# Node products in three fp32r passes, value copies on ScalarE, row sums on GpSimd, in a graph network kernel

## The reference, cut to what matters

```python
xn = layernorm(x)                                   # x: 12500 nodes x 256
h_src, h_dst = xn @ W_src, xn @ W_dst               # 4 heads of 64
a_src = sum_c(h_src * att_src); a_dst = sum_c(h_dst * att_dst)
e = leaky_relu(a_src[src] + a_dst[dst])             # 200000 edges, sorted by dst
alpha = segment_softmax(e, dst)
gat = prelu(layernorm(segment_sum(alpha * h_src[src], dst) + bias))
q, k, v = xn @ Wq, xn @ Wk, xn @ Wv                 # 8 heads of 32
Q, K = elu(q) + 1, elu(k) + 1
KV, Ks = sum_nodes(K^T v), sum_nodes(K)             # linear attention
mix = xn + mlp_and_norms((Q @ KV) / (Q . Ks), xn)
x = x + gat + mix
y = layernorm(x)
w = softmax(mean(y) @ Wr + br)                      # 8 experts
x = x + sum_e w[e] * ffn_e(y)                       # three 256x256 layers each
```

## Time and profile before

| | us |
|---|---|
| median of three runs | 4765.23 |
| lowest, highest run | 4764.68, 4774.9 |
| the profiled execution, its own time | 4775.0 |
| its span, first to last instruction | 4773.2 |
| TensorE busy | 4267.7 (89%) |
| VectorE busy | 3908.7 (82%) |
| ScalarE busy | 2264.6 (47%) |
| GpSimd busy | 1813.6 (38%) |
| mean granted TensorE clock | 0.944 of full speed |

### The profile page before, as it was taken

The page is one execution under the profiler, slowest core; times in us unless marked ns, Lnnn a source line. Parts: engine busy times, 40 slices in busy tenths (PEclk is TensorE's granted clock), DMA queues, the critical chain, the costliest instruction groups (busy, mean ns, idle before and its releaser), DMA issues. The chain is left out here.

```text
span 4773.2 us, 85825 instructions
## 1 busy us (share of the span) xinstructions
PE 4267.7 (89%) x22703; PEld 3319.2 (70%) x22704; DVE 3908.7 (82%) x10182; ACT 2264.6 (47%) x4194; POOL 1813.6 (38%) x1677
## 2 busy tenths in 40 slices
PE   8994888888888888888888885999999999999999
PEld 5663566666666656666666553788888888888888
DVE  7765888888888899888988986877778778778776
ACT  3331343343333343333333432666666666666666
POOL 0007777777777677776776750000000000000000
PEclk9996999998999899999998987999999999999999
DMA  5444766766666667666766663100000000000000
GB/s 189 152 135 138 202 194 202 210 197 190 198 209 199 191 195 216 200 197 187 217 204 191 195 184 110 38 28 15 28 28 14 28 22 21 28 15 28 28 15 19
DMA packets 440121, 603.08 MB, mean 126 GB/s; under 512 B 41544, under 2 KB 366672, under 8 KB 439888
## 3 DMA queue, kind: packets, MB, share of 16 engines
q1 hardware_dynamic: 360016, 378.46, 25.0%
q0 software_dynamic: 79872, 221.62, 17.3%
HBM read 312.66 MB, written 287.25 MB: 126 GB/s over the span
## 5 line engine op out<-in xcount | busy, mean ns | idle before, releaser
L817 POOL DMA_INDIRECT acc<-h_tab,strips x1664 | 1810.6, 1088 | 1028.5 <-issue 830.3
L1316 PE MATMUL ps<-acc 128*128 128x260 f32 x3328 | 991.9, 427 | 48.3 <-DVE acc L936 29.1
L951 DVE SCALAR_TENSOR_TENSOR acc<-acc,strips,ps 128x260 f32<-128x260 f32 x1664 | 796.5, 479 | 231.2 <-PE ps L1316 144.0
L1316 PEld LDWEIGHTS ps<-acc 128*128 128x128 f32 x3328 | 634.5, 208 | 195.5 <-issue 102.2
L936 DVE TENSOR_TENSOR acc<-acc 128x512 f32<-128x512 f32 x832 | 564.3, 683 | 0.0
L1818 ACT ACTIVATE exp<-ps,bn 128x512 f32<-128x512 f32 (+1 forms) x400 | 310.2, 776 | 510.9 <-PE ps L1885 507.3
L1135 ACT ACTIVATE strips<-ps 128x512 bf16<-128x512 bf16 x416 | 247.5, 595 | 428.7 <-PE ps L1292 424.7
L1883 PE MATMUL ps<-w_hi,b_hi 128*128 128x256 f32 x1568 | 444.9, 284 | 1.2 <-DVE exp L1722 1.2
L1885 PE MATMUL ps<-w_hi,b_lo 128*128 128x256 f32 x1568 | 443.6, 283 | 0.0
L1884 PE MATMUL ps<-w_lo,b_hi 128*128 128x256 f32 x1568 | 443.6, 283 | 0.0
L1730 DVE TENSOR_TENSOR a_lo<-exp,a_hi 128x512 fp32r<-128x512 f32 (+1 forms) x400 | 262.0, 680 | 183.4 <-ACT a_hi L1820 169.8
(11 more groups left out here) (256 smaller groups left out, 8116.7 us busy)
## 6 DMA issues: line engine op xcount, KB each, us to landing
side_tab<-acc SPq DMA_DIRECT2D x416, 520.0 KB
acc<-h_tab,strips POOLq DMA_INDIRECT x1664
strips<-xnt_tab SPq DMA_DIRECT2D x50, 512.0 KB
h_tab<-acc SPq DMA_DIRECT2D x25, 520.0 KB, 6.6
exp<-side_tab SPq DMA_DIRECT2D x100, 130.0 KB, 2.3
acc<-in_x SPq DMA_DIRECT2D x25, 512.0 KB, 5.3
base_tab<-acc SPq DMA_DIRECT2D x25, 512.0 KB, 3.2
xnt_tab<-acc SPq DMA_DIRECT2D x25, 512.0 KB, 6.0
```

The source lines that it names most:

```text
L817: pool.indirect_dma_start(G[s][:, b * GU + u], None, h_tab, bass.IndirectOffsetOnAxis(REC[s][:, b * GU + u, 0:1], 0)).then_inc(g_in[s], 16)
L951: nc.vector.scalar_tensor_tensor(A[:, (b % 2) * GU + u], A[:, (k - 1) % (2 * GU) if k else 2 * GU], smt[s][:, k:k + 1], ps[u][:, 0:MW], AL ...
L1316: nc.tensor.matmul(ps[u][:, 0:MW], S32[b % 2][:, u], G[s][:, b * GU + u], start=True, stop=True).then_inc(g_mm.sem, 1)
```

## The change

1. `products` multiplies high and low parts: xh·wh + xh·wl + xl·wh, each fp32r, so six products of each width instead of two per tile. ScalarE writes the high part of the transposed chunk right after the full one (which is still stored for the edge stage); VectorE writes the low part (`turned_low`), and the products wait for it. The weights are split once at the start: two copies on ScalarE, two subtractions on VectorE.
2. The copy of v into `VX` moves from VectorE to ScalarE, between relu k and h.
3. The addition for `XB` moves from VectorE to GpSimd, one per chunk as before. SyncE's base store waits for it, and so does the scaling two chunks on.
4. Order: the halves are transposed after tiles 0 and 1 instead of 1 and 2. The comparisons go from tile 0 to tile 3 and their counts into the following chunk. A segment is closed one chunk later, and the last segment and the joining come after tile 1 of the last chunk.
5. Memory: `acc` becomes a smaller area for weights (`keep`), one for the first stage and, in its place afterwards, one for the edge stage.

The diff, cut to its core:

```diff
             def scale(c):
                 s = c % 2
                 x_tr.wait(dve, c - 2)
+                x_base.wait(dve, c - 2)
...
                 ins.then_inc(x_norm.sem, 1)
-                x_norm.wait(dve, c)
-                used(dve, st_x[s], 16, c // 2)
-                nc.vector.tensor_tensor(XB[s], X[s], XN[s], ALU.add).then_inc(x_base.sem, 1)
+
+            def turned_low(c, k):
+
+                xt_ev.wait(dve, c, k + 1)
+                hk_mm.wait(dve, c - 2)
+                nc.vector.tensor_tensor(XTL[c % 2][:, k], XT[c % 2][:, k], XTH[c % 2][:, k].bitcast(f32),
+                                        ALU.subtract).then_inc(xt_lo.sem, 1)
...
+            for i, part in enumerate((slice(C_K, C_END), slice(C_H, C_K))):
+                dve.wait_ge(wch_set, i + 1)
+                nc.vector.tensor_tensor(WCL[:, :, part], wcat[:, :, part], WCH[:, :, part].bitcast(f32), ALU.subtract
+                                        ).then_inc(wcl_set, 1)
+            for k in range(KD):
+                turned_low(0, k)
             statistics(1)
             root(1)
             scale(1)
...
                     kv_mm.wait(dve, c - 1, t + 1)
                     k_act.wait(dve, c, t + 1)
-                    nc.vector.tensor_copy(VX[:, t, :, 0:P],
-                                          ps[4 + t % 2][:, D:2 * D].rearrange("p (g c) -> p g c", g=KD)
-                                          ).then_inc(v_ev.sem, 1)
                     nc.vector.scalar_tensor_tensor(KK[:, t], KE[:, t], 1.0, KR[:, t], ALU.min,
                                                    ALU.add).then_inc(k_dve.sem, 1)
-                    if t == 0:
+                    if t == 0 and c + 2 < NCH:
+                        statistics(c + 2)
+                    if t == 1 and c + 2 < NCH:
+                        root(c + 2)
+                    if t in (1, 2) and c + 1 < NCH:
+                        turned_low(c + 1, t - 1)
+                    if t == 2 and c + 2 < NCH:
+                        scale(c + 2)
+                    if c and c % SEG_TURNS == 0 and t == (1 if c == nseg * SEG_TURNS else CH - 1):
+                        segment(c // SEG_TURNS - 1)
+                        if c == nseg * SEG_TURNS:
+                            steps_joined()
+                    if t == CH - 1:
                         for k in compared(c):
                             compare(c // SEG_TURNS, k)
-                        if c + 2 < NCH:
-                            statistics(c + 2)
-                    if t == 1 and c + 2 < NCH:
-                        root(c + 2)
-                    if t == 2 and c + 2 < NCH:
-                        scale(c + 2)
-                    if t == CH - 1:
-                        if c % SEG_TURNS == SEG_TURNS - 1 and c < nseg * SEG_TURNS:
-                            segment(c // SEG_TURNS)
-                        if c == nseg * SEG_TURNS - 1:
-                            steps_joined()
...
                 hk_mm.wait(act, c - 2)
+                xt_lo.wait(act, c - 2)
                 x_tr.wait(act, c, k + 1)
-                nc.scalar.activation(XT[c % 2][:, k], ps[k][:, :], ACT.Copy).then_inc(xt_ev.sem, 1)
+                nc.scalar.activation(XT[c % 2][:, k], ps[k][:, :], ACT.Copy)
+                nc.scalar.activation(XTH[c % 2][:, k], ps[k][:, :], ACT.Copy).then_inc(xt_ev.sem, 1)
...
+            act.wait_ge(w_in, 16 * (KD + 4))
+            for i, part in enumerate((slice(C_K, C_END), slice(C_H, C_K))):
+                if i:
+                    act.wait_ge(fold_set, 4 * KD)
+                nc.scalar.activation(WCH[:, :, part], wcat[:, :, part], ACT.Copy).then_inc(wch_set, 1)
+                if i == 0:
+                    for k in range(KD):
+                        turned(0, k)
...
                     nc.scalar.activation(KR[:, t], ps[4 + t % 2][:, 0:D], ACT.Relu).then_inc(k_act.sem, 1)
+                    kv_mm.wait(act, c - 1, t + 1)
+                    nc.scalar.activation(VX[:, t, :, 0:P], ps[4 + t % 2][:, D:2 * D].rearrange("p (g c) -> p g c", g=KD),
+                                         ACT.Copy).then_inc(v_ev.sem, 1)
...
-                    if t in (1, 2) and c + 1 < NCH:
-                        turned(c + 1, t - 1)
+                    if t in (0, 1) and c + 1 < NCH:
+                        turned(c + 1, t)
...
             def products(c, t):

                 pc, pt = (c, t - 2) if t >= 2 else (c - 1, t + 2)
-                xt_ev.wait(pe, c)
+                xt_lo.wait(pe, c)
...
                 for lo, hi, bank in ((C_H, C_K, 2), (C_K, C_END, 4)):
+                    o = ps[bank + t % 2][:, 0:hi - lo]
                     for k in range(KD):
-                        ins = nc.tensor.matmul(ps[bank + t % 2][:, 0:hi - lo], XT[c % 2][:, k, t * P:(t + 1) * P],
-                                               wcat[:, k, lo:hi], start=k == 0, stop=k == KD - 1)
+                        xh, xl = (x[c % 2][:, k, t * P:(t + 1) * P] for x in (XTH, XTL))
+                        wh, wl = WCH[:, k, lo:hi], WCL[:, k, lo:hi]
+                        nc.tensor.matmul(o, xh, wh, start=k == 0, stop=False)
+                        nc.tensor.matmul(o, xh, wl, start=False, stop=False)
+                        ins = nc.tensor.matmul(o, xl, wh, start=False, stop=k == KD - 1)
...
-            pe.wait_ge(w_in, 16 * (KD + 4))
-            pe.wait_ge(fold_sum, 2 * KD)
+            pe.wait_ge(wcl_set, 2)
...
-                    if t in (1, 2) and c + 1 < NCH:
-                        turned(c + 1, t - 1)
-                    if t == 2:
+                    if t in (0, 1) and c + 1 < NCH:
+                        turned(c + 1, t)
+                    if c and t == (0 if c == nseg * SEG_TURNS else 2):
                         if record_turn(c) is not None:
                             rec_ev.wait(pe, record_turn(c))
-                        for k in compared(c):
-                            counts(c // SEG_TURNS, k)
+                        for k in compared(c - 1):
+                            counts((c - 1) // SEG_TURNS, k)
...
+                for c in range(NCH):
+                    s = c % 2
+                    x_norm.wait(pool, c)
+                    pass_on(pool, "pool")
+                    used(pool, st_x[s], 16, c // 2)
+                    nc.gpsimd.tensor_tensor(XB[s], X[s], XN[s], ALU.add).then_inc(x_base.sem, 1)
```

More of the change, by code:

```diff
@@ L138, in build, with rounded @@
         early = ExitStack()
-        acc_t = early.enter_context(nc.sbuf_tensor("acc", [P, 25000], f32))
-        strip_t = early.enter_context(nc.sbuf_tensor("strips", [P, 12288], f32))
+        keep_t = early.enter_context(nc.sbuf_tensor("keep", [P, 4360], f32))
+        strip_t = early.enter_context(nc.sbuf_tensor("strips", [P, 8192], f32))
         work_t = early.enter_context(nc.sbuf_tensor("work", [P, 12088], f32))
+        first = ExitStack()
+        proj_t = first.enter_context(nc.sbuf_tensor("proj", [P, 16840], f32))
+        def rounded(name, n):
+            return first.enter_context(nc.sbuf_tensor(name, [P, KD * n], f32r))[:, :].rearrange("p (k n) -> p k n", k=KD)
+        XTH, XTL = [[rounded(f"xt_{v}{s}", CT) for s in range(2)] for v in ("hi", "lo")]
+        WCH, WCL = rounded("wc_hi", C_END), rounded("wc_lo", C_END)
         ps = [es.enter_context(nc.psum_tensor(f"ps{i}", [P, 512], f32)) for i in range(8)]
@@ L165, in build @@
         RSQ = 12
-        r1 = Region(acc_t)
+        r1 = Region(keep_t)
         kvx = r1.take(KD, P + HH)
@@ L173, in build @@
         w2 = r1.take(2 * KD, D)
-        r2_from = r1.at
+        r1 = Region(proj_t)
         wcat = r1.take(KD, C_END)
         wdst = r1.take(KD, D)
-        fold = r1.take(2, KD, D)
         X = [r1.take(CH, D) for _ in range(2)]
@@ L183, in build @@
         KE = r1.take(CH, D)
+        fold = KE.rearrange("p (s k) d -> p s k d", k=KD)
         KR = r1.take(CH, D)
@@ L205, in build @@
         kv_all, kv_cp, ad_set = sem("kv_all"), sem("kv_cp"), sem("ad_set")
+        wch_set, wcl_set, xt_lo = sem("wch_set"), sem("wcl_set"), stage("xt_lo", 2)
         x_v = a["x"].rearrange("(c t p) d -> c p t d", t=CH, p=P)
@@ L248, in compared @@
             return range(KC * j // SEG_TURNS, KC * (j + 1) // SEG_TURNS) if i < nseg else ()
[L250 to L254, removed]
         r4 = Region(strip_t)
@@ L280, in build @@
         bnt = [r4.take(16) for _ in range(3)]
-        BTQ, BTU, QQ, QR = (r4.take(KD, CT) for _ in range(4))
-        MTT, MN, MLT = QQ, QR.rearrange("p k n -> p (k n)").rearrange("p (t d) -> p t d", t=CH), QR
         rm = Region(work_t)
@@ L426, in record_turn @@
             r, j = divmod(c, SEG_TURNS)
-            return r - 2 if j == 0 and 0 <= r - 2 < AHEAD - 1 else None
+            return r - 2 if j == 1 and 0 <= r - 2 < AHEAD - 1 else None
         def project_sync(sp):
@@ L544, in project_vector @@
                 nc.vector.tensor_tensor(heads(fold[:, 0, k]), wcat[:, k, 0:MW].rearrange("p (h c) -> p h c", c=HB)[:, :, 0:HB - 1],
```

(29 more changed lines are left out.)

9 lines of the change are left out of this document (4 added, 5 removed).

## The result

| us | median | lowest to highest | executions |
|---|---|---|---|
| before | 4766.3 | 4764.68 to 4774.9 | 5 |
| changed | 4741.15 | 4736.96 to 4744.9 | 5 |

The ratio is 0.9943 (95% interval 0.993 to 0.9957), 25.2 us less. That is faster. It lies inside the range for 8 in 10, which reached to 4750 for rival 1's sake, but outside the forecast's own 4715 to 4731, and 18.6 us above the predicted 4722.5. It is the place of rival 1. The profiled execution took 4740.85 us.

What follows compares the result with a forecast made beforehand. TensorE was taken to bound the first stage. Products -47.0, start +2.2, end +0.9 and GpSimd's addition +1.2 made -42.7 us, so 4765.2 became 4722.5; own range 4715 to 4731, 8 in 10 from 4712 to 4750.

Steps and rivals of the forecast that it cites:

- rival 1: First stage: GpSimd's addition blocks tile 3's sum on VectorE, 14 to 36 us lost, 4735 to 4757 us; chance 0.24.
- The products: First stage, TensorE: a tile's products fall from 2.61 to 2.12 us, the chunk to 11.48; -47.0 us over 24 periods.
- the unknown: GpSimd's addition beside VectorE: length taken as 1.8 us, tile 3's sum taken to start first; +1.2 us.
- VectorE, ScalarE and SyncE's queue: Steady chunks: VectorE 8.2 and ScalarE 7.7 of 11.48 us, low parts and stores in time; nothing counted.
- The walk of the chunk: VectorE's order timed from a chunk's first product: low parts 1.0 us early, addition and tile 3's sum both ready near 12.0.
- Start: First chunk: products start near 17.1 us, tile 1 at 23.5, tile 2 at 26.6 against 24.40; +2.2 us.
- End: Last chunk: TensorE's 2.0 us stand goes, but joining delays tile 3's sum to 7.6 us, against 4.7; net +0.9 us.

Runs made afterwards that it cites:

- the plain products' run: Changed kernel with the products put back to plain f32, high and low parts still made but unused; first gather of the edge stage at 367.79 us, chunk 13.44 us.
- the repeat with the wait: Changed kernel with GpSimd's addition waiting for tile 3's sum, run again on the last chip; 4716.58 us, ratio to before 0.9895, first gather of the edge stage at 320.21 us.

## Why the prediction was right and wrong

**The products: right.** A chunk without the hold takes 11.45 us, forecast 11.48; from one key-value sum to the next are 2.57 (2.12 + 0.45). With the hold out of the way the marks are 320.2 to 321.3, so 46 to 47 us against before, where the sum without the unknown was 43.9. The 2 to 3 us more come from the end, below.

**VectorE, ScalarE and SyncE's queue: right.** No low part, turned half or store is what TensorE waits for in any steady chunk, and moving the work gave nothing where the products didn't shrink (the plain products' run). The walk of the chunk put tile 3's sum and the addition both at 12.0; in the trace they are 0.1 us apart.

**Start: the step was right in part.** The first product is at 17.18 (forecast 17.1) and tile 1's at 23.49 (23.5):

```profile
23.49 0.57 PE L712 MATMUL ps<-wc_hi,xt_hi 128*128 128x264 f32 x1
...
23.86 0.42 PE L713 MATMUL ps<-wc_lo,xt_hi 128*128 128x264 f32 x1
24.08 0.42 PE L714 MATMUL ps<-wc_hi,xt_lo 128*128 128x264 f32 x1
...
27.53 0.37 PE L712 MATMUL ps<-wc_hi,xt_hi 128*128 128x264 f32 x1
```

Tile 2's came at 27.53 instead of 26.6: I had counted 3.1 us for tile 1 and what follows it, and it took 4.0. Tile 1's steps of 264 columns are 0.22 us apart instead of 0.124, though the granted clock reads 1.00 there. That spacing doesn't explain all of it. In the repeat with the wait they are 0.12 apart after the same stand of 1.33 us, and tile 2 still came 3.8 us after tile 1, because TensorE waited for tile 0's sum. This sum stands behind a small instruction that GpSimd's second addition (22.85 to 25.21) holds, and that takes 0.10 us in the kernel before:

```profile
23.44 1.81 DVE L579 TENSOR_SCALAR work<-work 128x13 int32<-128x13 int32 x1
```

**End: mis-sized.** Tile 3's sum ends at 333.9, 7.6 us after tile 1's products, as forecast. But the 4.7 us set against them were counted from the end of tile 2's products, not of tile 1's. In the kernel before, the key-value sum of tile 1 (the one with 84 rows, for the last chunk has 212 nodes) stands behind the products that end at 353.3, and each key-value sum stands behind the next tile's products:

```profile
345.62 2.77 PE L687 MATMUL ps<-acc 128*128 128x264 f32 x8
...
353.33 0.61 PE L674 MATMUL ps<-acc 84*128 84x129 f32 x4
```

So tile 1's products end at 345.62 + 2.61 = 348.2. From the start of tile 2's products to the mark are 367.09 - 350.72 = 16.4 us before and 320.21 - 303.89 = 16.3 with the wait: the joining between the sums cost nothing on balance, and the 2.0 us for which TensorE had stood were gained. The end is -2.0, not +0.9. With the start at +2.6 and the periods at -47.4 that gives the 46.9 us of this version.

**The failed step** is the case taken for the unknown: "If the sum starts first, only the comparisons wait, VectorE runs later, the next sum is ready before the scaling ends and is first again. I take that case, at 0.05 us a chunk". It took the race as correcting itself. It doesn't: the hold makes TensorE wait, tile and scaling shift by the same 1.17 us, and the next chunk meets the same 0.08 us. A VectorE late with extra work did put the sum first, as argued, but the hold doesn't make it late against TensorE, and after each of the four additions where the sum won, the next addition was ahead again. So the term is 19 x 1.17 = 22.2 us in place of 1.2. The length was mis-sized too: 1.8 taken, 2.39 measured.

Put together, from the forecast of 42.7 us go 21.0 for the hold and 0.9 for the start (3.1 instead of 2.2), and 2.9 for the end and 0.4 for the periods come on top: 24.1, and the mark moved by 24.25. That the miss wasn't larger is luck, for the wrong end term covered 2.9 us of it. Rival 1 had the mechanism and the price by length; the sum starts beside the addition and ends with it, where I had written that it would start as the addition ends. Its chance of 0.24 was too low for two events that the walk itself had put at the same 12.0.

The Trainium skill, "SBUF — State Buffer", section "Who interferes with whom", has the rule by which rival 1 works: two-input VectorE work and GpSimd's reading exclude each other for the whole instruction. The traces agree, with 2.59 against 0.42 us, and 0.94 when the addition is cut in four. The Trainium skill, "GPSIMD Engine Reference", section "Elementwise — side-by-side cycle accounting", would make the addition 2.25 us, by estimate; it measures 2.39 here.

## What to carry to other kernels

When work moves to GpSimd, ask which VectorE instruction is next to start in each period, not only whether both engines have room: a race between two starts can fall the same way every time. Put the GpSimd instruction behind the last urgent one by a wait, or cut it in pieces; here the wait cost nothing and gave 17.6 us. A rival whose only defence is "the other will be first" within a margin smaller than the walk's error deserves half of the chance.

## What the runs showed that I had not expected

- The hold works both ways. An addition that starts first holds the folding 2.58 us; when two foldings start first, the addition takes 3.37 instead of 2.39 us.
- It isn't limited to instructions with two inputs from SBUF. It takes in comparisons with a single wide input (two in 2.90 us instead of 0.77) and the one of 13 columns above (1.81 instead of 0.10), but not a copy from PSUM (0.42 inside the addition) nor, at the start, reductions of one SBUF input (0.41 each). What sets the two groups apart wasn't tested.
- A GpSimd addition has a fixed share: 256 columns take about 0.82 us in a row of four (with VectorE's sum between them), 512 1.30, 768 1.86, 1024 2.39.
- 80 ns of order, repeated 19 times, were worth as much as half of the faster products. In two executions of the changed kernel it fell alike at all 23 additions behind the start, with the same four exceptions.
